# A delta-rule attention block on one core: the triangular inverse kept in one PSUM bank, the norms broadcast through DRAM, and every engine's order rewritten

## What is computed

```python
q = _l2norm(einsum('bsd,de->bse', hidden_states, Wq).reshape(b, s, H, D))
k = _l2norm(einsum('bsd,de->bse', hidden_states, Wk).reshape(b, s, H, D))
v = einsum('bsd,de->bse', hidden_states, Wv)
q, k, v = (_causal_dwconv_silu(a, conv) for a, conv in ...)        # 4 taps over time, then silu
beta = sigmoid(einsum('bsd,dh->bsh', hidden_states, Wb))
g_forget = -exp(A_log) * softplus(g_lin + dt_bias)
# delta rule, step by step in time
Sst = Sst * exp(gt)[..., :, None]
err = vt - einsum('bhk,bhkv->bhv', kt, Sst)
Sst = Sst + bt[..., None, None] * kt[..., :, None] * err[..., None, :]
ot = einsum('bhk,bhkv->bhv', qt, Sst)
# then: rms norm of ot, times sigmoid(gate), times Wo, added to x
```

## Time and profile before

| | |
|---|---|
| runs | 942.79 us median of 3 (942.67 to 944.27) |
| the profiled execution | 945.35 us, its span on the core 943.3 us |
| PE, DVE, ACT, POOL busy | 859.7, 827.8, 677.0, 142.4 us |
| matrix products | 20394 records; one fp32 product of the program is two records |

### The profile page before, as it was taken

How to read it: one execution, slowest core, us unless ns; L and a number is a source line. 1 busy time by engine, 2 the same in 40 slices (tenths; PEclk the granted TensorE clock), 3 DMA queues, 4 the chain that set the end, 5 groups by cost and what they waited for, 6 DMA issues and landing times.

```text
span 943.3 us, 45531 instructions
## 1 busy us (share of the span) xinstructions
PE 859.7 (91%) x20394; PEld 607.8 (64%) x20394; DVE 827.8 (88%) x1740; ACT 677.0 (72%) x1652; POOL 142.4 (15%) x307
## 2 busy tenths in 40 slices
PE   4889689999999999999999999999999997888876
PEld 3634356766766667666667666666666666777765
DVE  6677899999999999999999999999999899768634
ACT  3377758888888788888888788878887786545431
POOL 8000111111111111111111111011111011111100
PEclk9999889999999999999999999999999899988888
DMA  6200111100000011300001112000000000000001
GB/s 160 68 0 4 43 34 34 46 14 15 15 4 18 21 33 34 90 14 4 14 3 34 35 34 79 15 15 15 15 15 15 14 15 13 16 5 3 4 1 44
DMA packets 29079, 24.84 MB, mean 26 GB/s; under 512 B 4627, under 2 KB 24277, under 8 KB 28885
## 3 DMA queue, kind: packets, MB, share of 16 engines
q1 hardware_dynamic: 28884, 21.94, 8.5%
HBM read 20.82 MB, written 1.11 MB: 23 GB/s over the span
## 4 chain that ended last, share of the span: by engine, by line
PE 53%; DVE 33%; ACT 8%; issue 5%; DMA 0%; SPq 0%; DVEq 0%; ACTq 0%
PE psum L883 7%; PE psum L941 6%; PE psum L1025 6%; DVE pairs L1362 5%; PE psum L916 4%; DVE kq L1344 4%; PE psum L898 3%; PE psum L990 3%; PE psum L997 3%; DVE state L1334 3%; PE psum L983 3%; PE psum L976 3%; PE psum L893 3%; DVE ks L1346 2%; DVE qkv L1320 2%
## 5 line engine op out<-in xcount | busy, mean ns | idle before, releaser
L883 PE MATMUL psum<-hT,gw 128*128 128x512 f32 x384 | 185.8, 609 | 0.8 <-ACT hT L553 0.8
L1315 DVE SCALAR_TENSOR_TENSOR qkv<-pad,chan,qkv 128x512 f32<-128x512 f32 x192 | 144.1, 792 | 0.1
L883 PEld LDWEIGHTS psum<-hT,gw 128*128 128x128 f32 x384 | 71.7, 193 | 85.3 <-issue 83.1
L1344 DVE TENSOR_TENSOR kq<-kq,tot 128x512 f32<-128x512 f32 x160 | 109.3, 683 | 8.7 <-PE psum L916 8.7
L1362 DVE COPY_PREDICATED pairs<-masks,psum 128x256 f32<-128x256 uint8 x192 | 101.3, 527 | 15.1 <-PE psum L916 9.1
L916 PE MATMUL psum<-kq,ks 128*32 128x32 f32 x5120 | 77.7, 201 | 18.0 <-ACT oT L704 11.8
L614 ACT ACTIVATE tmat<-psum 128x128 f32<-128x128 f32 x128 | 35.9, 280 | 74.9 <-PE psum L941 74.7
L941 PEld LDWEIGHTS psum<-fmat,pairs 32*32 32x32 f32 x4096 | 46.0, 107 | 58.3 <-issue 48.7
L622 ACT ACTIVATE rr<-rl 64x512 f32<-64x512 f32 x128 | 80.3, 627 | 1.7
L462 POOL TENSOR_TENSOR tot<-dec 128x256 f32<-128x256 f32 x32 | 30.4, 951 | 317.9 <-ACT dec L718 298.8
L916 PEld LDWEIGHTS psum<-kq,ks 128*32 128x32 f32 x5120 | 58.6, 114 | 27.8 <-ACT oT L704 14.3
(11 more groups left out here) (171 smaller groups left out, 1907.8 us busy)
## 6 DMA issues: line engine op xcount, KB each, us to landing
bb<-beta_rows SPq DMA_DIRECT2D x32, 256.0 KB, 3.3
gw<-in_L_attn_Wq SPq DMA_DIRECT2D x16, 128.0 KB, 2.3
gw<-in_L_attn_Wk SPq DMA_DIRECT2D x16, 128.0 KB, 2.4
gw<-in_L_attn_Wv SPq DMA_DIRECT2D x16, 128.0 KB, 2.3
gwo<-in_L_attn_Wo SPq DMA_DIRECT2D x4, 512.0 KB, 6.6
x<-in_L_attn_hidden_states SPq DMA_DIRECT2D x4, 256.0 KB, 4.7
gfb<-in_L_attn_Wfb SPq DMA_DIRECT2D x16, 64.0 KB, 2.2
ggb<-in_L_attn_Wgb SPq DMA_DIRECT2D x4, 256.0 KB, 5.3
```

What stands on the lines that cost most here:

```text
L883: last = eng.matmul(two(bank[to]), gw[:, t, kt, hh * D:(hh + 1) * D], two(hT[:, kt])[:, :, h * PW:(h + 1) * PW], start=(kt == 0), stop=(kt ...
L1315: last = eng.scalar_tensor_tensor(out=piece(t, i), in0=src, scalar=tap_weight(t, tap, i), in1=piece(t, i), op0=ALU.mult, op1=ALU.add)
L1344: eng.tensor_tensor(half(kq[:, p], h, 1), half(kq[:, p], h, 1), lower.rearrange("p (a n o) -> p a n o", a=1, o=1).broadcast_to((P, 2, nb, ...
```

## The change

- **Inverse.** `tmat`, `tt` and `fmat` are gone. All natural products of levels 0 to 4 are written or accumulated into one PSUM bank (`T_BANK`) with `start=False`, so that bank holds the inverse so far. ACT copies it out after each level (`copy_natural`, 128x128), and copies each Y product as well (`copy_y`), where DVE added it to an identity. DVE transposes 128x128 straight from PSUM. The bank serves one chunk at a time: `first_natural` of a chunk waits for the last transpose of the chunk ahead. POOL places the two diagonal blocks (`place_blocks`), and ACT puts the last corner in.
- **32x32 tiles.** The diagonal, the last level's product, the last Y product and the last product of the inverse are done with 32-wide tiles where they had 64.
- **Norms.** `channel_sums` writes four groups of 32 partitions, 256 columns wide. ACT does one `Ln` and one `Exp` of 128x256 into `root`; SP stores four rows of it to `norm_rows` in DRAM, waits for the store, and loads it back broadcast to 128 partitions as `rr` (512 KB).
- **Moved to ScalarE.** The first taps of q and k, and the keeping of level 5.
- **Level 0.** The decays of level 0 are done as two products of 512 columns from `kraw`, where there were one of 1024 and one of 512.
- **Orders.** `slot(t)` of every engine is rewritten; banks are dealt out anew; PE works on item t+6 and chunk t-3 in slot t as well.

```diff
-L_BANK = (7, 3, 0, 0, 6, 1)
-Y_BANK = (None, 3, 4, 1, 5, 4)
-TM_BANK = (None, 0, 3, 4, 5)
+L_BANK = (4, 7, 7, 2, 3, 2)
+Y_BANK = (None, 3, 7, 2, 3, 2)
+T_BANK, T5_BANK, DG_BANK, KT_BANK, VR_BANK, U_BANK, O_BANK, OT_BANK, WO_BANK, S_BANK, GT_BANK, Q_BANK, K_BANK, NN_BANK, V_BANK, F_BANK = 0, 3, 5, 1, 4, 7, 6, 4, 6, 3, 3, 1, 5, 6, 7, 2
...
             def channel_sums():
                 for t in range(2):
-                    last = eng.matmul(bank[NN_BANK][rows(t), :], ones[:, 0:C], sq[:, t], start=True, stop=True)
+                    for b in range(B):
+                        last = eng.matmul(bank[NN_BANK][quarter(t, b), 0:PW], ones[:, 0:QUARTER],
+                                          sq[:, t, b * PW:(b + 1) * PW], start=True, stop=True)
...
             def diagonal(p):
                 for u in range(G):
                     for b in range(B):
-                        last = eng.matmul(cell(bank[DG_BANK][:, 0:UC], b, u), ks[:, p, tokens(b, u)],
-                                          kraw[:, 1, tokens(b, u)], start=True, stop=True)
+                        for j in range(2):
+                            at = tokens32(b, u, j)
+                            last = eng.matmul(block_of(bank[DG_BANK][:, 0:UC], b, u, j), ks[:, p, at],
+                                              kraw[:, 1, at], start=True, stop=True)
...
+            def inverse_natural(p, l):
+                ...
+                            last = eng.matmul(half(strip(bank[T_BANK][quarter(b, j)], u), h, 0), left,
+                                              y[quarter(b, j), u, j * per:(j + 1) * per],
+                                              start=False, stop=(l == NL - 2), skip_group_check=True)
...
-            def inverse_sum(l):
-                h = LEVELS[l]
-                lower = [half(v, h, 0) for v in (fmat[:, l - 1], id64[:, :])]
-                return eng.tensor_tensor(lower[0], lower[1], blocks(bank[Y_BANK[l]][:, 0:HC], h), ALU.add)
+            def copy_y(l):
+                return eng.activation(ysum[:, l - 1], bank[Y_BANK[l]][:, 0:HC], ACT.Copy)
...
-                return eng.transpose(tt[:, p], tmat)
+                return eng.transpose(turned[:, p], bank[T_BANK][:, 0:HC])
...
+                if 0 <= im2 < NCK:
+                    after(root_ready, im2 + 1)
+                    eng.dma_start(norm_rows.rearrange("a (q n) -> (a q) n", q=2 * B), root[0:P:QUARTER, :]).then_inc(norm_stored, 16)
+                if 0 <= n1 < NCK:
+                    if n1 == 0:
+                        store_beta()
+                    if n1 >= 29:
+                        after(kb_ready, n1 - 1)
+                    eng.dma_start(bb[:, n1 % 2], beta_rows[n1:n1 + 1, :].broadcast_to((P, UN))).then_inc(in_beta[n1 % 2], 16)
+                if 0 <= im2 < NCK:
+                    landed(norm_stored, im2 + 1)
+                    eng.dma_start(rr[:, :, :].rearrange("p t n -> p (t n)"), norm_rows.broadcast_to((P, 2 * UN))).then_inc(in_norm, 16)
```

More of the change, by code:

```diff
@@ L95, in build @@
         sdec = sb("sdec", [P, B, UN])
-        tmat = sb("tmat", [P, UC])[:, :]
+        corner = sb("corner", [P, 2])
+        natural = sb("natural", [P, 2, HC])
+        turned = sb("turned", [P, 2, HC])
         rows1, rows2 = rs[:, 0:P], rs[:, P:2 * P]
@@ L380, in _ @@
+            for t in range(-2, NCK + 4):
+                slot(t)
             for i in range(2):
@@ L432, in _ @@
                 level_mask(l, h - 1, 2 * h, -1)
-            for l in range(1, NL):
-                last = eng.tensor_copy(fmat[:, l - 1], id64[:, :])
-            last.then_inc(pool_chain, 1)
+            eng.memset(inverse[:, :, :], 0.0)
+            eng.tensor_copy(start_turned, id64[:, :]).then_inc(pool_chain, 1)
             eng.wait_ge(pool_chain, 6)
@@ L733, in slot @@
[L733 to L742 removed]
+                    copy_last(q).then_inc(inverse_ready, 1)
@@ L943, in block_products @@
-                return last
-            def inverse_y(l):
-                h = LEVELS[l]
-                o = bank[Y_BANK[l]][:, 0:HC].rearrange("p (u n t) -> p u n t", u=G, t=h)
-                if l < NL - 1:
-                    return block_products(o, l, nmat[:, l], tmat, 0)
-                for u in range(G):
-                    for b in range(B):
-                        last = eng.matmul(o[rows(b), u], cell(nmat[:, l], b, u)[0:QUARTER], half(cell(tmat, b, u), h, 0)[0:QUARTER],
-                                          start=True, stop=True)
-                return last
```

1117 lines of the change are left out of this document (608 added, 509 removed).

## The result

The changed kernel took 896.15 us in the median of four runs (891.17 to 912.06), the kernel before 942.73 us on the same chip: a ratio of 0.9484 with the 95% interval [0.9431, 0.9537]. It is faster by 47 us where 32 were forecast, and the time lies in the range. So statements on sizes are checked against both profiles. Medians are of all runs, ratios leave out runs over 1.5% above the kernel's fastest: here the 912.06, without which the median is 894.68.

The account below looks back on a forecast made before the run. PE and DVE were taken to share the path, with PE alone setting the new slot. Full slots -39, filling +14 and end -7 gave -32 us, from a median of 942.8 to 911 us; range 884 to 938.

Parts of the forecast that it names:

- PE's sum: PE work in a full slot: cheaper diagonal, last level, last products and channel sums, together -1.13 us.
- The last products: Last Y product and last product of the inverse on PE, 0.59 us each: -0.2 each, -0.4 together.
- the wait: PE's 0.47 us wait inside a full slot for ACT's copy of `oT`; 0.35 counted as gained.
- all hidden: Rival, 17%: load lands in 3.3 us, sums run on four groups, last products halve; slot 23.1, 889 us.
- DVE and ACT: Work per full slot: DVE falls from 24.2 to about 20.7 us, ACT goes from 20.5 to about 20.8.
- Full slots: Slots with all engines busy: from 25.0 to 23.5 us each, -39 us over 26 slots.
- all else on PE is the same work: Step in PE's full-slot count: beyond the listed savings of 1.13 us, PE's work stays unchanged.
- Filling: Slots before the full ones: +14 us (0 to +38), from rounds +9, beta's store +3, lower clock +2.
- the five rounds: Norms rounds in the filling slots: 13.9 us each against 12.1 before, +9 us (0 to +17).
- The end: Slots 27 to 31: less work and shorter transposes shorten the chain, about -1.4 each, -7 us (0 to -15).
- ACT as partner bound: Rival, 13%: late short copies on ACT cost PE 0.8 us a slot; slot 24.3, 935 us.
- slower: Rival, 11%: each of nine inverse copies on ACT keeps PE 0.3 us; slot 26.2, 988 us.

Follow-up runs that it names:

- both profiles: Profiled executions of two series of the unmodified changed kernel: 912.06 us in the first (median 896.15), 900.77 us in the second (median 903.29).
- the load twice: Changed kernel plus a second 512 KB load of the norms' rows per slot, into a DRAM buffer nobody reads; 945.18 us.
- the base run: The changed kernel measured once more, nothing changed, as reference for the follow-up kernels; 903.29 us, ratio 0.955 to the kernel before.

## Why the prediction was right, and where its sizes were off

The sign, the order of the terms and the bound were right: two engines shared the path, the change took work from both, and PE alone bounds the full slots now. The terms of the two profiles add up to -33.5 and -44.6 us against the profile before; that the first is so near to -32 is partly luck, as the terms show:

- **PE's sum.** -1.13 forecast, -1.50 measured. The last products were mis-sized: I took 0.2 off each of 0.59, and they overlap with their neighbours to 0.26. The other places are within 0.1: sums and last level 0.74 for 0.60, diagonal 0.10 for 0.13. With the wait gone (0.47 for 0.35), a calm slot is 23.02, not 23.5, as the rival "all hidden" had it (23.1).
- **DVE and ACT.** From the window 200 to 400, some 21.0 and 21.1 us of a slot of about 23.2; forecast 20.7 and 20.8. Here the sums held. PE waits for none of ACT's copies in a calm slot.
- **The new term, and the step that failed.** Full slots were to gain 39 us; the calm slot alone gives 26 x 1.82 = 47.3, and the profiles gave 34.0 and 35.3. The difference is the 12 to 13 us by which the stalls grew. I costed the norms' load by its landing alone, 5.0 us and hidden. It landed in 4.1 and was hidden, and PE stood still for it all the same: with the weights behind it 12.7 us of this stretch went, and with a second such load 36 came in. The step "all else on PE is the same work" is true and was not enough: PE also needs its instructions. The two errors nearly cancel in this term, so that -39 looks better than it was.
- **Filling.** +14 forecast, +16.3 and +9.8 measured at chunk 0, from other parts than forecast. An undisturbed round took 12.0 to 13.1 us, not 13.9 (the terms give 13.8), since the store's landing and the load came in 5.7, not 7.2. So the five rounds, +9 in the forecast, cost next to nothing: the first three took 39.3 and 37.4 us, and 38.6 before (46.50 to 85.06). Nearly all came from the round with beta's store, 21.3 and 20.1 us, where the kernel before took 9.85 (a timeline of its PE, and the earlier trace rows):

```profile
85.06 1.08 PE L898 MATMUL psum<-sq,ones 128*64 128x512 f32 x4 [0.69 <-ACT sq L711]
```

Beta's store was costed at 3 and cost 6.4 at chunk 0. That the sum is near +14 is luck. The clock in the filling window is 0.76 (before 0.85), lower as named.
- **The end.** -7 forecast, -16.7 and -19.2 measured between chunks 26 and 31. The mechanism (a shorter chain) was right, but the larger part was overlooked: the clock. A wait of PE and windows of the kernel before in one of its last slots; then the stretch from chunk 26 to 31 before, and in both profiles after:

```profile
827.97 0.45 PE L931 MATMUL psum<-id,pairs 32*32 32x32 f32 x32 [2.05 <-DVE pairs L1362]
...
826.00:828.00 2.00, 0.03 (x4) 0.03 (x5) 2.00 (x5) 2.00 (x9) 1.21 (x1) 1.00 0.00 0
830.00:834.00 4.00, 4.00 (x66) 3.63 (x63) 2.91 (x5) 0.00 (x0) 0.00 (x0) 0.50 0.00 0
```
```profile
793.20:904.50 111.30, 96.37 (x2803) 80.71 (x2800) 78.48 (x180) 54.55 (x179) 13.55 (x29) 0.86 0.03 8
...
775.50:870.10 94.60, 84.13 (x2836) 69.12 (x2832) 64.06 (x146) 61.57 (x211) 13.62 (x23) 0.95 0.03 10
...
767.70:859.80 92.10, 82.79 (x2843) 67.96 (x2832) 62.16 (x143) 61.36 (x211) 14.33 (x23) 0.96 0.04 10
```

Before, PE stood still for 2.05 us in such a slot, waiting for DVE's copy into `pairs`, and then ran at half clock; the last four of these slots have 0.83 to 0.85. After, single slots are at 0.91 or 0.92 and the others at 1.00. An estimate from these rows: the time that the lower clock costs, if PE is busy all through it, is the missing share times the length, up to 0.14 x 111.3 = 15.6 us before and 0.05 x 94.6 and 0.04 x 92.1, about 5 and 4 us, after. That makes up to 11 and 12 us of the 16.7 and 19.2; the other 6 and 7 are about what the shorter chain was forecast to give. That this is the cause of the size fits the rows, but was not tried by itself.
- **ACT as partner bound, and "slower".** Neither happened, and the runs say how far off they were: 0.7 us more on ACT is free, with 2.2 us more PE waits 1.1 a slot for its copies. Nine copies at 0.3 each, the slower case, showed nothing of it.

By the Trainium skill, page "DMA: Bandwidth & Descriptors", section "Anatomy of one DMA", the load was estimated at 3.2 us; the trace has 4.1 in the median, between that and my 5.0.

Open: whether the bytes or the many small packets of the loads hold the fetches back, whether the number of PE's instructions or their pace decides, and how much the gate's and the output's weights would give if they too came behind the norms' load.

## What to carry to other kernels

A transfer that is hidden can still cost: when several loads of one queue fill the DMA engines at once, look for waits "<-issue" in the middle of a dense step and for gaps between instruction packets, and let the loads follow one another before you reduce them. Cutting a product into narrower tiles buys PE time with more instructions in less time; its worth depends on whether they arrive. And on an in-order queue, nothing that waits for another engine belongs ahead of a load on which a short loop turns.

## What was not expected of the hardware

- Instructions come in DMA packets of 16 KB through the whole run, in the median every 4.3 us in full slots. In all 11 stalls over 0.4 us of the changed kernel from 150 to 760 us, and all 22 with the load twice, a packet came late (gap 5.7 to 10.2 us) and PE resumed 1.2 to 1.7 us after its end.
- A 512 KB load more per slot, read by nobody, cost some 40 us in 32 items, 1.2 to 1.3 us each.
- A standstill of PE of 2.53 us was followed by some 3.4 us at 1.2 GHz (granted clock 0.50), and in the kernel before one of 2.05 us by 0.50 from 830 to 834. Shorter ones went both ways: after the 2.16 us that ended at 534.00, the window 535 to 542 of the same profile has 0.51, after the 1.68 us that ended at 437.33 the window 437 to 441 has 1.00. In the base run the clock was 0.65 in the 4 us after a stall of 1.13 us, and 1.00 after one of 1.26 us.
